# Lines' first blocks: row numbers read in place, a down product moved behind the first projections, sums in pairs of tiles

## The reference, cut to what matters

```
x = x + 0.5 * ffn(layernorm(x))
x = x + attn(layernorm(x))
x = x + 0.5 * ffn(layernorm(x))
```

```
y = sum over the 2 chosen experts e of weight_e * ((silu(x We1_e + be1) * (x We3_e + be3)) We2_e + be2)
z = (silu(x ws1 + bs1) * (x ws3 + bs3)) ws2 + bs2
ffn = y + z
```

```
L = [p1_i * p2_j - p1_j * p2_i for the 6 pairs i < j];  L = L / max(norm(L), 1e-12)
attn = softmax(causal(L_q . J L_k / sqrt(6))) @ (x W_v + b_v);  out = attn @ W_o + b_o
```

## Time and profile before

| what | us |
|---|---|
| median of 3 runs (1151.79 to 1153.61) | 1151.9 |
| the profiled execution | 1152.4 |
| its span, first to last instruction | 1150.7 |
| busy: PE / ACT / DVE / POOL | 1031.4 / 871.0 / 772.6 / 460.1 |
| mean granted TensorE clock (1 is full) | 0.982 |

### The profile page before, as it was taken

One profiled execution on the slowest core, in us unless ns is written; L12 is line 12 of the kernel. 1 busy time (PEld: TensorE's weight loads), 2 busy tenths in 40 slices (PEclk: granted clock), 3 DMA queues, 4 the chain that ended last, 5 costly groups with the idle time before them and its releaser, 6 DMA issues.

```text
span 1150.7 us, 23627 instructions
## 1 busy us (share of the span) xinstructions
PE 1031.4 (90%) x7535; PEld 561.0 (49%) x7537; DVE 772.6 (67%) x1565; ACT 871.0 (76%) x1250; POOL 460.1 (40%) x675
## 2 busy tenths in 40 slices
PE   8998999978888787998899898989899988999996
PEld 4466999945555121222122222222224568999854
DVE  6898787758996524434254657467768678778866
ACT  4326777735887999999999999999997236777610
POOL 1003666457730423422221323431413335677755
PEclk8999999999998899999999999999999999999998
DMA  8911555445766221020201122120100944566654
GB/s 287 276 55 53 171 167 168 151 124 168 225 201 190 68 69 52 11 65 10 65 10 37 35 69 78 34 70 19 48 1 28 317 144 148 164 189 184 173 173 151
DMA packets 125717, 133.79 MB, mean 116 GB/s; under 512 B 13224, under 2 KB 111888, under 8 KB 125616
## 3 DMA queue, kind: packets, MB, share of 16 engines
q1 hardware_dynamic: 109056, 90.95, 24.9%
q0 software_dynamic: 14448, 39.47, 12.3%
q10 hardware_dynamic: 2112, 2.10, 0.5%
HBM read 80.43 MB, written 52.04 MB: 115 GB/s over the span
## 4 chain that ended last, share of the span: by engine, by line
PE 26%; ACT 24%; issue 15%; DVE 10%; POOL 3%; DVEq 1%; DMA 1%; ACTq 0%; POOLq 0%
ACT wide L2026 23%; PE banks L2398 6%; PE banks L1910 6%; PE banks L2323 4%; PE banks L2410 3%; POOL f_region L1349 2%; PE banks L1884 2%; PE banks L2332 2%; DVE x_res L1603 1%; PE banks L2386 1%; DVE wide L1630 1%; DVEq L2606 1%; PE banks L1924 1%; DVE attn_lines_parts L202 1%; DVE f_xnt L2617 1%
## 5 line engine op out<-in xcount | busy, mean ns | idle before, releaser
L2026 ACT ACTIVATE wide<-banks 128x1536 f32<-128x1536 f32 (+1 forms) x384 | 492.5, 1490 | 4.4 <-PE banks L1884 3.1
L1910 PE MATMUL banks<-wide,attn_attend_v_now 128*32 128x512 f32 (+3 forms) x2560 | 288.2, 541 | 2.4 <-POOL wide L2036 2.2
L2036 POOL TENSOR_SCALAR_AFFINE_SELECT wide<-wide 128x256 f32<-128x256 f32 (+1 forms) x320 | 115.8, 391 | 390.3 <-ACT wide L2026 387.8
L1884 PE MATMUL banks<-attn_attend_q_now,attn_attend_k_now 32*128 32x512 f16 (+3 forms) x1280 | 150.7, 354 | 57.0 <-ACT wide L2026 55.1
L1884 PEld LDWEIGHTS banks<-attn_attend_q_now,attn_attend_k_now 32*128 32x128 f16 x1280 | 38.7, 91 | 292.3 <-ACT wide L2026 247.8
L659 POOL DMA_INDIRECT f_region<-xn_rows,f_token_of x79 | 78.5, 994 | 125.1 <-DVE f_token_of L890 82.6
L2081 DVE COPY sums<-banks 128x512 f32<-128x512 f32 x32 | 22.1, 691 | 135.2 <-PE banks L1910 135.0
L2398 PE MATMUL banks<-f_xnt 128*128 128x128 f32 x752 | 101.5, 278 | 10.1 <-DVE f_more L2624 6.3
L2086 DVE RECIPROCAL below<-below 128x512 f32<-128x512 f32 x32 | 107.3, 3353 | 1.1
L2398 PEld LDWEIGHTS banks<-f_xnt 128*128 128x128 f32 x752 | 91.3, 191 | 15.3 <-ACT f_xnt L2476 9.6
L2506 POOL DMA_INDIRECT last_rows_in<-xn_rows,f_spare x72 | 70.3, 976 | 66.9 <-DVE f_stage L2567 23.7
(11 more groups left out here) (366 smaller groups left out, 1784.4 us busy)
## 6 DMA issues: line engine op xcount, KB each, us to landing
y_half<-f_xnt SPq DMA_DIRECT2D x94, 128.0 KB
y_slots<-wide SPq DMA_DIRECT2D x79, 128.0 KB, 1.7
attn_v<-f_more SPq DMA_DIRECT2D x32, 256.0 KB
attn_attend_v_now<-attn_v SPq DMA_DIRECT2D x32, 256.0 KB, 3.4
x_res<-L_attn_x SPq DMA_DIRECT2D x8, 512.0 KB, 7.7
xn_rows<-f_w_all SPq DMA_DIRECT2D x8, 512.0 KB, 5.1
attn_q<-attn_lines_q_out SPq DMA_DIRECT2D x8, 512.0 KB, 3.5
attn_k<-attn_lines_k_out SPq DMA_DIRECT2D x8, 512.0 KB, 4.1
```

The lines of the kernel that those rows point to most:

```text
L1884: last = pe.matmul(score[i % SLOTS][:, j, column:column + columns(u)], k_now[rows, kt * P:(kt + 1) * P], q_now[rows, qc * QW + c0:(qc + 1) ...
L1910: last = pe.matmul(out_bank[qc][rows, c0:QW], v_now[:, kt, rows], probs[:, place, column:column + columns(u)], start=(kt == 0), stop=(u == ...
L2026: act.activation(probs_flat[:, at:at + width_of[i]], score_flat[i % SLOTS][:, 0:width_of[i]], ACT.Exp, scale=SCALE).then_inc(sem.exp_done, 1)
L2036: pool.affine_select(out=part, in_=part, compare_op=ALU.is_ge, fill=0.0, base=0, pattern=[[0, part.shape[1]], [1, P]], channel_multiplier= ...
```

## The change

- POOL: for blocks 0 to 3 the copy of row numbers is left out, and the DMAs take the numbers from `core.slots` itself. A `sem_inc` stands in its place.
- DVE, blocks 0 to 2: the sums are done in pairs of tiles (`combine_pair`): choice 0 and 1 of tiles 0 and 1 and their two `bn_stats`, then the same for tiles 2 and 3. In block 2 `measure_lines` stands between the pairs. `combined` and `first_added` count 2 for each block.
- DVE: `multiply(1)` and `add_shared(0)` stand behind `invert` of block 0, `add_shared(1)` behind `invert` of block 2, b_o's addition at the end of block 2.
- PE: `shared_down(1)` stands behind block 0's projections and `project_bias` behind block 1's; block 0's third projection waits for `multiply(1)`, whose banks it takes over.
- ACT: a square root of one column (`hint`) behind the late silus; in block 1 the points and values of block 0 are copied ahead of `normalize`, tiles 0 and 1 ahead of the root and tiles 2 and 3 behind it.
- PE, end of the first feed-forward: `keep_busy(12)`, twelve bf16 matmuls of 128 x 512 on a constant into bank 7, which nobody reads.

```diff
@@ ffn, tensor
             expert_steps(pe, emit, 3)
+            keep_busy(12)
@@ lines, gpsimd
                 if after(n, 2):
-                    pool.wait_ge(sem.combined, n - 1)
-                pool.tensor_copy(rows_of[:, q, :, :], core.slots[:, bass.ds(n * BT, BT), :]).then_inc(sem.picked, 1)
+                    pool.wait_ge(sem.combined, 2 * (n - 1))
+                here = isinstance(n, int) and n < 4
+                if here:
+                    pool.sem_inc(sem.picked, 1)
+                else:
+                    pool.tensor_copy(rows_of[:, q, :, :], core.slots[:, bass.ds(n * BT, BT), :]).then_inc(sem.picked, 1)
...
+                        rows = core.slots[:, n * BT + j, k:k + 1] if here else rows_of[:, q, j, k:k + 1]
@@ lines, tensor
                 last.then_inc(sem.turned, 1)
-                if isinstance(n, int) and n == 0:
-                    shared_down(1)
-                if isinstance(n, int) and n == 1:
-                    project_bias()
...
                 for j in range(BT):
                     if after(n, 1):
                         pe.wait_ge(sem.value_ready, BT * (n - 1) + j + 1)
+                    if isinstance(n, int) and n == 0 and j == 2:
+                        pe.wait_ge(sem.late_prod, LATE)
...
+                if isinstance(n, int) and n == 0:
+                    shared_down(1)
+                if isinstance(n, int) and n == 1:
+                    project_bias()
@@ lines, scalar
         act.wait_ge(sem.filled, 2)
+        act.activation(hint[:], stats.eps[:], ACT.Sqrt)
...
+            early = isinstance(n, int) and n == 1
+            if early:
+                points_and_values(n - 1, 1 - q, r if q else r - 1, (0, 1))
             if has_block(n, 0):
                 stats.take_root(act, n, q)
+            if early:
+                points_and_values(n - 1, 1 - q, r if q else r - 1, (2, 3))
...
-            if has_block(n, 1):
+            if has_block(n, 1) and not early:
                 points_and_values(n - 1, 1 - q, r if q else r - 1)
@@ lines, vector
         def step_block(n, q, r):
-            if has_block(n, 0):
+            first = isinstance(n, int) and n <= 2
+            if first:
+                stats.wait_turn(dve, n)
+                combine_pair(n, q, r, 0)
+                if n == 2:
+                    measure_lines(n - 1, q)
+                stats.sum_up(dve, n, q, combine_pair(n, q, r, 1))
+            elif has_block(n, 0):
                 combine(n, q, r)
-            if has_block(n, 2):
+            if has_block(n, 2) and not first:
                 measure_lines(n - 1, q)
-            if has_block(n, 0):
-                dve.wait_ge(sem.combined, n + 1)
+            if has_block(n, 0) and not first:
+                dve.wait_ge(sem.combined, 2 * (n + 1))
                 stats.sum_up(dve, n, q)
-                if isinstance(n, int) and n == 0:
-                    multiply(1)
-                if isinstance(n, int) and n == 2:
-                    dve.wait_ge(sem.b_projected, 1)
-                    dve.tensor_tensor(b_o[:], bank[6][:, 0:D], b_o[:], ALU.add).then_inc(sem.b_ready, 1)
...
                 stats.invert(dve, n, q)
-                if isinstance(n, int) and n < LATE:
-                    add_shared(n)
+                if isinstance(n, int) and n == 0:
+                    multiply(1)
+                    add_shared(0)
+                if isinstance(n, int) and n == 2:
+                    add_shared(1)
             if has_block(n, 2):
                 split_lines(n - 1, q)
+            if isinstance(n, int) and n == 2:
+                dve.wait_ge(sem.b_projected, 1)
+                dve.tensor_tensor(b_o[:], bank[6][:, 0:D], b_o[:], ALU.add).then_inc(sem.b_ready, 1)
...
+        def combine_pair(n, q, r, pair):
+
+            tiles = (2 * pair, 2 * pair + 1)
+            for j in tiles:
+                dve.wait_ge(fetched[q * BT + j], 16 * TOPK * (r + 1))
+                last = add_rows(n, q, j, 0)
+            last.then_inc(sem.first_added, 1)
+            dve.wait_ge(sem.first_added, 2 * n + pair + 1)
+            for j in tiles:
+                last = add_rows(n, q, j, 1)
+            last.then_inc(sem.combined, 1)
+            dve.wait_ge(sem.combined, 2 * n + pair + 1)
+            return stats.take_parts(dve, n, q, tiles)
```

More of the change, by code:

```diff
@@ L185, in tile, with take_parts, sum_up @@
         return self.x[:, bass.ds(t, 1), :].rearrange("p o d -> p (o d)")
-    def sum_up(self, dve, n, q):
+    def take_parts(self, dve, n, q, tiles):
+        for j in tiles:
+            last = dve.bn_stats(self.parts[:, q, j, :], self.tile(n * BT + j))
+        return last
+    def sum_up(self, dve, n, q, last=None):
         sem, done = self.sem, [0]
@@ L196, in sum_up @@
         parts, mean, gap, var = self.parts[:, q], self.mean[:, q], self.gap[:, q], self.var[:, q]
-        if after(n, 2):
-            dve.wait_ge(sem.staged, n - 1)
-            dve.sem_inc(sem.stat_turn, 1)
-        for j in range(BT):
-            last = dve.bn_stats(parts[:, j, :], self.tile(n * BT + j))
+        if last is None:
+            self.wait_turn(dve, n)
+            last = self.take_parts(dve, n, q, range(BT))
         step(last)
@@ L208, in sum_up, with wait_turn @@
         dve.tensor_tensor(var, gap, var, ALU.add).then_inc(sem.var_ready, 1)
+    def wait_turn(self, dve, n):
+        if after(n, 2):
+            dve.wait_ge(self.sem.staged, n - 1)
+            dve.sem_inc(self.sem.stat_turn, 1)
     def take_root(self, act, n, q):
@@ L1304, in lines @@
     v_stored, fetched = ring_semaphores(nc, f"{tag}_v_stored", 2), ring_semaphores(nc, f"{tag}_fetched", 2 * BT)
-    stats = Statistics(x, sb, sem)
+    stats, hint = Statistics(x, sb, sem), sb("hint", [P, 1])
     WEIGHTS = 16 * 10
@@ L1348, in step @@
                     for k in range(TOPK):
+                        rows = core.slots[:, n * BT + j, k:k + 1] if here else rows_of[:, q, j, k:k + 1]
                         pool.indirect_dma_start(out=back[:, q, j, k, :], out_offset=None, in_=y_slots,
-                                                in_offset=bass.IndirectOffsetOnAxis(ap=rows_of[:, q, j, k:k + 1], axis=0)
+                                                in_offset=bass.IndirectOffsetOnAxis(ap=rows, axis=0)
                                                 ).then_inc(fetched[q * BT + j], 16)
@@ L1505, in features, with points_and_values @@
                                    ).then_inc(signal, 1)
-        def points_and_values(n, q, r):
+        def points_and_values(n, q, r, tiles=range(BT)):
             if after(n, 2):
@@ L1590, in step_block, with add_rows @@
                 stats.invert(dve, n, q)
-                if isinstance(n, int) and n < LATE:
-                    add_shared(n)
+                if isinstance(n, int) and n == 0:
[3 more added lines that the diff above has]
+                    add_shared(1)
             if has_block(n, 2):
                 split_lines(n - 1, q)
+            if isinstance(n, int) and n == 2:
+                dve.wait_ge(sem.b_projected, 1)
+                dve.tensor_tensor(b_o[:], bank[6][:, 0:D], b_o[:], ALU.add).then_inc(sem.b_ready, 1)
+        def add_rows(n, q, j, k):
+            t = n * BT + j
+            return dve.scalar_tensor_tensor(stats.tile(t), back[:, q, j, k, :], core.weight[:, k, bass.ds(t, 1)], stats.tile(t),
+                                            ALU.mult, ALU.add)
+        def combine_pair(n, q, r, pair):
+            tiles = (2 * pair, 2 * pair + 1)
+            for j in tiles:
+                dve.wait_ge(fetched[q * BT + j], 16 * TOPK * (r + 1))
+                last = add_rows(n, q, j, 0)
+            last.then_inc(sem.first_added, 1)
+            dve.wait_ge(sem.first_added, 2 * n + pair + 1)
+            for j in tiles:
+                last = add_rows(n, q, j, 1)
+            last.then_inc(sem.combined, 1)
+            dve.wait_ge(sem.combined, 2 * n + pair + 1)
+            return stats.take_parts(dve, n, q, tiles)
         def combine(n, q, r):
@@ L1599, in combine @@
                 for j in range(BT):
-                    t = n * BT + j
                     if k == 0:
                         dve.wait_ge(fetched[q * BT + j], 16 * TOPK * (r + 1))
-                    last = dve.scalar_tensor_tensor(stats.tile(t), back[:, q, j, k, :], core.weight[:, k, bass.ds(t, 1)], stats.tile(t),
-                                                    ALU.mult, ALU.add)
+                    last = add_rows(n, q, j, k)
                 if k == 0:
-                    last.then_inc(sem.first_added, 1)
-                    dve.wait_ge(sem.first_added, n + 1)
-            last.then_inc(sem.combined, 1)
+                    last.then_inc(sem.first_added, 2)
+                    dve.wait_ge(sem.first_added, 2 * (n + 1))
+            last.then_inc(sem.combined, 2)
         def stepper(n, ahead):
@@ L1832, in sync @@
             sp.wait_ge(stored, 16 * BT * BLOCKS // 2)
-        sp.wait_ge(lines_sem.combined, BLOCKS)
```

(1 more changed line is left out.)

## The result

| | before | after |
|---|---|---|
| median of 12 runs each, in turn on one chip | 1152.55 | 1150.08 |
| lowest and highest | 1151.09 to 1154.62 | 1147.93 to 1152.24 |
| profiled execution / its span | 1152.4 / 1150.7 | 1148.11 / 1146.4 |
| mean granted TensorE clock of it | 0.982 | 0.986 |

The ratio is 0.9978, its 95% interval 0.9968 to 0.9987: 2.5 us faster (1.5 to 3.7), where 1.65 was forecast. The time itself, 1150.3 forecast, came out as 1150.08. That this is so close is luck in part: the forecast started from a median of 1151.9, and the kernel before took 1152.55 in these runs, which hides 0.65 of the 0.8 by which the gain was forecast too small.

A forecast was written before the change was run, and what follows sets the result against it. Start-up until DVE's block 3 was the limit, its bound passing from POOL's fetches to PE: 282.29 - 280.58 = 1.71, minus 0.05 of barrier, 1.65 us gained, so 1150.3 us; range 1148.7 to 1152.5.

The forecast's parts named there:

- (a): POOL's fetches without the row-number copy: block 0's come 0.24 us earlier (bounds 0 and 1.0), 0.65 saved at later block borders.
- (b): DVE, block 0: five adds behind the last tile become three, two bn_stats already done; variance starts at 249.87, before at 251.69.
- the cover: DVE free at 246.9 to 247.3, last tile at 247.23: thin margin for the first pair, giving out at 246.9.
- (c): ACT: the square-root table load leaves the path between block 0's variance and reciprocal; gain 1.36 us, bounds 0 to 1.36.
- (d): PE, end of first feed-forward: twelve dummies cost 0.05 us at the barrier, avoid 1.5 at half clock and transposes 0.5 late.
- (e): PE: with shared_down(1) behind block 0's projections, these start at 255.63, 5 us earlier; 3.46 of that goes to shared_down(1).
- (f): PE's project_bias behind block 1's projections ends at 280.18; DVE idles some 2 us for it, block 3 starts at 280.58.
- R1: Larger gain: block 3 does not wait for PE, only DVE's own time counts, up to 3.7 us, 1148.2; chance 0.12.
- R2: A part does nothing: table load still behind the variance, 1151.6, or half clock after the barrier, 1150.8; chance 0.12.
- R3: Slower: PE's clock falls at the start of the projections, costing 2.0 us, 1152.3, or up to 1154.8; chance 0.14.
- The step that failed: Attention and second FFN behind the last line block move one for one; block 3 to end changes by at most 1 us.

The follow-up runs named there:

- e8: The changed kernel without the square-root hint, so ACT loads the table behind block 0's variance again; 1153.51 us, ratio 1.0015 to the kernel before.
- e7: e1 with four and five dummy matmuls around block 0's transposes and DVE's b_v copy moved behind add_shared(0); 1150.08 us, ratio 0.9979 to the kernel before.
- e2: The changed kernel with shared_down(1) back in front of block 0's projections, behind its transposes; 1155.38 us, ratio 1.003 to the kernel before.
- e1: The changed kernel with project_bias ahead of block 1's projections and add_shared(1) ahead of block 2's second pair; 1149.39 us, ratio 0.9977 to the kernel before.
- e4: The changed kernel run again with no edit; 1149.47 us, ratio 0.9984 to the kernel before.
- e12: e7 plus eight dummies ahead of each block's feature transposes from block 1, fifteen between attention's second and third strips; 1149.28 us, ratio 0.9962 to the kernel before.
- e5: e2 with dummy matmuls in PE's waits, four ahead of block 0's transposes and eleven ahead of block 1's; 1152.05 us, ratio 0.9999 to the kernel before.
- e6: The changed kernel with four, five and five dummy matmuls in PE's waits around block 0's and 1's transposes; 1149.55 us, ratio 0.9983 to the kernel before.

## Why the prediction was right, point by point

**(a) Row numbers in place.** The first issue started 0.83 us behind the barrier's release, against 1.02 before: 0.19 where I put 0.24. At the block borders the 1.0 shrank to the 0.30 that lies between any two issues: 0.7 saved, where I took 0.65. What it gained in blocks 1 and 2 bought nothing, as said: the chain leaves the fetches after block 0's rows. No run took (a) out alone.

**(b) Pairs.** Variance forecast at 249.87, measured 249.74. The range's warning about the cover came true through another wait, b_v's copy waiting for the last weight; it moved block 3 by 0.7 between two profiles of one kernel, a term that was missing from the range.

**(c) The hint.** 1.36 forecast, 1.33 between e8 and after. The load row shows 1.28 and the square root followed the variance by 0.19 (249.74 to 249.93). The Trainium skill (ScalarE: Activation LUTs, What ACT_TABLE_LOAD costs) adds 1.38 of drain to the 1.28; here ACT had been idle before the load, and the measured 1.33 leaves no room for that part, so the measurement decides. What I did not price was what stands behind the hint: in e8's profile the clock falls without it, and the edit is worth 3 to 4 us and not 1.4.

**(d) keep_busy.** Clock full from 234.8 on, shared_up 1.5 us sooner, transposes 0.45 sooner, barrier not later. Right in each row against the first profile; in the medians it can't be seen.

**(e), (f) The order and the bias.** The forecast stands in brackets. Projections at 255.46 (255.63), block 1's transposes at 267.67 (267.85), next projections at 270.21 (270.39), the bias's matmuls over at 280.0 (280.18), DVE idle 1.79 for it (2), block 3 at 280.38 (280.58). The bound passed from POOL's fetches to PE, as the chain shows. That the second profile put block 3 at 46.49 behind the barrier and not at 45.82 means that the start-up saved 1.0 to 1.6 us, and the forecast's 1.7 is the upper end.

**The rivals.** R1 was not the case: DVE waited for PE. e7 shows that its size was right, block 3 at 44.3 against a forecast for it of 43.8 (278.6 less 234.8); its time, 1148.2, did not come with it. R2 was not the case. R3 was not the case in the kernel after, which passes at 0.91 and 1.51 us of idle time; it was in e8 and e2, and for e1 in part. I gave it 0.14 from a gap of 2.5 us that had held and one of 3.7 that had not. No such edge exists between the two: the clock fell behind 2.2 us of idle time in e8 and behind 1.3 followed by 1.5 in e1, and held behind 1.6 followed by 1.5 in e4. That the forecast came out right on this point is luck in part. The Trainium skill (TensorE: Matmul & The Clock Gate, What's actually happening) says that the gate's phase differs from run to run. No run shows the phase itself, but what they show agrees: two executions of the kernel after had their 1.2 GHz stretches at different places (besides attention's start, near 312 us in the first; from 296 to 303 and near 342 in e4), and its runs spread over 4.3 us, the slower ones at a lower clock (1147.9 at 0.987, 1152.2 at 0.980).

**The step that failed** is the claim that everything behind block 3 moves one for one, with the bound I set myself of 1 us. That distance shrank by 2.4 us in the profiled pair (868.4 to 866.0), and it was 866.1 to 870.9 over the profiles of e1 to e8 and e12. Of the 2.4, 1.67 was the clock in the last line block; it is fixed in its work and not in its clock. The 0.8 by which the gain of 2.5 exceeds the 1.65 lies inside the interval, and I can't say whether it is chance, or that after more seldom meets the 1.2 GHz level in its last line block; that would take profiles of many runs. Also open is whether e12 gains anything over the kernel after, and if so whether from the 1.5 to 2 us of e7's order or from the held clock: against e7 its row has 1.7 less in "to scores" and 2.3 less in attention, against after nothing in either, and after itself with the clock held was run only on the disturbed chip.

## What to carry to other kernels

Find the one wait that ends last in a stage, say what is late next, and the gain of a start-up change follows from rows: here to within 0.1 us in one profile, and 0.7 off in another, by a wait for the last weight that the rows of before do not show. Where PE becomes that bound, its idle gaps have to be priced too: a gap that costs nothing by the timeline can put the next microseconds of matmuls at half speed, in one execution and not in the next, and an edit that shortens such a gap (a table load moved away) can earn more than its own length. Dummy matmuls were cheap where they ended ahead of what PE waited for (e5, e6), and dear where they began after the clock had fallen (e12); a gain in the medians was shown only where the clock had fallen without them (e5 against e2).

## What the runs showed of the hardware

- An indirect fetch costs POOL 0.95 us and 0.30 to the next; the first behind a barrier starts 0.83 us after PE's first matmul, even with nothing in front of it, and tile 3's rows landed 2.76 us after its last issue.
- The 1.2 GHz level came behind a gap of 2.2 us in front of eight transposes in e8, and behind 1.28 and 1.51 around them in e1; the 2.4 GHz level held over 0.91 and 1.51 in after, 1.58 and 1.51 in e4, and 2.52 in front of them in before. Ahead of the last block's feature transposes the same gap of 2.74 ended in either level. Lost in e8: 3.85 us for 1.33 us of delay.
- Fifteen bf16 matmuls of 128x512, most of them at 1.2 GHz, took 5.96 us in e12; five at the full level took 1.25 in e7.
- Two DMA issues of SP took 0.97 us in one execution of the kernel after and 2.34 in the other (e4). The last weight's transfer landed 1.4 us later behind the barrier for it (9.97 against 8.58), which moved block 3 by 0.7.
